# Involution stage: every second tap's multiply made one VectorE instruction of 1024 columns instead of two of 512

## The reference

```
r = relu(((x @ Wr + br) - mean) * rsqrt(var + eps) * gamma + beta)   # 16 channels
w = (r @ Ws + bs)                                   # 16 groups x 9 weights at each pixel
xi = x @ Wi + bi                                    # 64 channels, then padded by 1
patches[i, j] = xi_padded[i:i+32, j:j+32]           # 9 shifted copies
out = sum over the 9 taps of (w * patches), taken in the reference's own order of channels
x = x + out
```

## Time and profile before

| what | value |
|---|---|
| median of 3 runs | 677.94 us (677.34 to 678.18) |
| the profiled execution: its own time | 679.21 us |
| the profiled execution: span from first to last instruction | 677.4 us |
| PE busy | 647.1 us, 96% of the span |
| DVE busy | 552.7 us, 82% |
| ACT busy | 290.9 us, 43% |
| POOL busy | 172.4 us, 25% |
| mean granted TensorE clock | 0.980 of full speed |

### The profile page before, as it was taken

The page is one execution under the profiler, slowest core; times in us unless marked ns, Lnnn a source line. Parts: engine busy times, 40 slices in busy tenths (PEclk is TensorE's granted clock), DMA queues, the critical chain, the costliest instruction groups (busy, mean ns, idle before and its releaser), DMA issues.

```text
span 677.4 us, 14867 instructions
## 1 busy us (share of the span) xinstructions
PE 647.1 (96%) x6176; PEld 258.9 (38%) x6176; DVE 552.7 (82%) x904; ACT 290.9 (43%) x383; POOL 172.4 (25%) x156
## 2 busy tenths in 40 slices
PE   7868999899999999999999999999999999999995
PEld 7433333333333333333333334433444444444442
DVE  5699876979987988896486697848988888888885
ACT  3753622322322322132202310043688778778761
POOL 2100320008201900370032030321334234235230
PEclk9979999899999999999999999997999999999998
DMA  9930000000000000000000000000032132132132
GB/s 331 209 64 1 2 1 1 1 1 1 3 1 1 2 1 1 1 1 2 1 1 15 1 1 1 2 9 9 10 70 48 40 71 48 40 71 48 40 71 63
DMA packets 55119, 21.76 MB, mean 32 GB/s; under 512 B 51250, under 2 KB 51988, under 8 KB 55060
## 3 DMA queue, kind: packets, MB, share of 16 engines
q1 hardware_dynamic: 54772, 20.66, 12.4%
q10 hardware_dynamic: 288, 0.21, 0.1%
HBM read 10.38 MB, written 8.39 MB: 28 GB/s over the span
## 4 chain that ended last, share of the span: by engine, by line
PE 77%; DVE 12%; issue 1%; ACT 1%; DVEq 0%; ACTq 0%
PE conv L683 35%; PE conv L738 12%; PE att L754 11%; PE att L473 5%; PE conv L649 5%; DVE xpad L1199 3%; PE att L552 3%; PE att L564 2%; PE att L725 2%; DVE stats L1302 2%; DVE comb L1288 1%; PE att L531 1%; DVE x L1257 1%; DVE x L1264 1%; DVE x L1508 1%
## 5 line engine op out<-in xcount | busy, mean ns | idle before, releaser
L683 PE MATMUL conv<-xpad,comb 64*64 64x512 f32 x2592 | 290.2, 595 | 2.8 <-DVE x L1264 2.7
L1508 DVE TENSOR_TENSOR x<-conv,x 128x512 f32<-128x512 f32 x288 | 178.0, 683 | 24.1 <-PE conv L738 22.8
L683 PEld LDWEIGHTS conv<-xpad,comb 64*64 64x64 f32 x2592 | 98.5, 134 | 170.7 <-issue 160.1
L1288 DVE SCALAR_TENSOR_TENSOR comb<-experts,wsel,comb 128x576 f32<-128x576 f32 (+1 forms) x138 | 113.5, 888 | 5.2 <-ACT comb L866 4.8
L738 PE MATMUL conv<-rstack,wse 98*128 98x512 f32 x288 | 95.7, 437 | 1.7 <-DVE xin L1297 0.9
L866 ACT ACTIVATE comb<-experts,wsel 128x576 f32<-128x576 f32 (+2 forms) x49 | 35.2, 769 | 109.2 <-PE conv L683 69.7
L754 PE MATMUL att<-x,cmp 64*32 64x512 f32 x1280 | 80.5, 601 | 0.0
L738 PEld LDWEIGHTS conv<-rstack,wse 98*128 98x128 f32 x288 | 48.5, 190 | 70.6 <-DVE x L1508 63.9
L1199 DVE SCALAR_TENSOR_TENSOR xpad<-att,x 128x1024 f32<-128x1024 f32 x46 | 54.0, 1216 | 20.6 <-PE att L531 20.4
L1645 POOL TENSOR_TENSOR x<-x,xin 128x1024 f32<-128x1024 f32 x15 | 35.9, 2396 | 111.4 <-ACT x L1008 111.4
L876 ACT ACTIVATE x<-conv,bias 128x512 f32<-128x512 f32 x40 | 25.2, 681 | 83.8 <-PE conv L683 83.8
(11 more groups left out here) (187 smaller groups left out, 604.6 us busy)
## 6 DMA issues: line engine op xcount, KB each, us to landing
x<-in_x SPq DMA_DIRECT2D x32, 256.0 KB, 5.1
out<-comb SPq DMA_DIRECT2D x30, 256.0 KB, 3.2
rstack<-rstack SPq DMA_DIRECT2D x16, 128.0 KB, 3.8
experts<-in_We SPq DMA_DIRECT2D x1, 1152.0 KB
out<-comb SPq DMA_DIRECT2D x4, 128.0 KB, 2.2
wide<-in_c_wide SPq DMA_DIRECT2D x1, 192.0 KB, 6.6
x<-in_c_sum SPq DMA_DIRECT2D x1, 160.0 KB
small<-in_c_small ACTq DMA_DIRECT2D x1, 142.5 KB, 3.8
```

The lines of the kernel that those rows point to most:

```text
L683: last = nc.tensor.matmul(conv[own[to], h, HW * rows:HW * rows + HW], comb[own[rows], q % 2, n, tap(t)], xpad[own[rows], 2 * (q % 2) + n, ...
L1288: v.scalar_tensor_tensor(comb[:, q % 2, n, cols], experts[:, e, cols], wsel[:, p % 2, j + QP * n, e:e + 1], comb[:, q % 2, n, cols], ALU.m ...
L1508: v.tensor_tensor(img(prod[i])[:, rows, :], img(conv[:, unit, :])[:, rows, :], xip[s][:, kh + 16 * h:kh + 16 * h + 16, kw:kw + W], ALU.mul ...
```

## The change

`product` gets a second form for the odd taps (1, 3, 5 and 7). It waits until both halves of the unit are full, multiplies all 1024 columns in one instruction and raises `prod_ready` by 2 at its end. Even taps keep their two instructions of 512 columns. Nothing on the other engines is changed.

```
                 if not first:
                     eng.wait_ge(sum_done, (k - 1) * len(ROUNDS) + ROUND_OF[i] + 1)
+                if i % 2:
+                    eng.wait_ge(exp_full, 2 * e + 2)
+                    v.tensor_tensor(img(prod[i]), img(conv[:, unit, :]), xip[s][:, kh:kh + H, kw:kw + W], ALU.mult).then_inc(prod_ready, 2)
+                    return
                 for h in range(2):
                     rows = slice(16 * h, 16 * h + 16)
                     eng.wait_ge(exp_full, 2 * e + h + 1)
```

## The result

The changed kernel takes 680.88 us (median of 6 runs, 680.44 to 681.82), the kernel before 677.95 us (677.34 to 678.18): the ratio is 1.0049, 95% interval 1.0037 to 1.0060. That is +2.93 us; +2.65 was forecast. The profiled execution took 681.82 us with a span of 680.0, 2.6 more on both counts than the one before.

The account below looks back on a forecast made before the run. TensorE's own order was taken to bound the kernel. 2.15 us for pairs 2 to 14, 0.20 for pairs 1 and 15 and 0.3 for pair 0 gave 677.94 + 2.65 = 680.6 us, range 678.8 to 682.7.

Parts of the forecast that it names:

- Which engine sets the period: Middle pairs: TensorE's own order sets the 12.73 us; VectorE matters only where TensorE runs into one of its waits.
- The price of the merged product: VectorE, odd taps: a merged product takes 1.14 us of its time in place of 1.20, saving about 0.065 each.
- D: Time from start to release of a merged product on VectorE, taken as 1.215 us, bounds 1.162 to 1.330.
- The release: Tap 3's upper half comes 0.535 us later, so both tap 5 matmuls wait: next group +0.165 us a pair.
- the formula D - 1.05: How far the group after tap 5 moves in a middle pair, in us; +0.165 as forecast.
- The other odd taps: Taps 1, 5 and 7: later releases cost nothing while D stays under about 1.54; at least 0.33 us to spare.
- A middle pair's term: Pairs 2 to 14: each 0.165 us longer through the wait at tap 5, 2.15 us in all 13.
- Pair 1: Second pair of the last stage, where tap 1 and tap 3 are both late: forecast to cost +0.10 us.
- the start side: A merged product starts only when both halves are full: at tap 3 0.5 us is spare, so cost nothing.
- Faster, by VectorE's rate: Rival: VectorE's time is all on the path, 64 x 0.065 = 4.2 us go, 673.8 us; chance 0.07.
- No change, with ScalarE setting xi: Rival: ScalarE's release of xi's first load hides the lateness in middle pairs, 678.4 us; chance 0.13.
- Slower still, by stalls at tap 3 and tap 7: Rival: D over 1.54 makes tap 3 and tap 7 stall too, 684.9 us; chance 0.05.

Follow-up runs that it names:

- the long filler ahead of tap 7: Kernel before, plus a VectorE memset of 128x272 ahead of tap 7: 677.96 us, ratio 1.0000.
- The cut after 24 rows: Kernel before, with tap 3 cut after 24 image rows in place of 16, still two instructions: 678.12 us, ratio 1.0000.

## Why the prediction was right

*Which engine sets the period.* It was read from the waits and the chain, not from busy shares: VectorE was 87% busy in a middle pair (11.12 of 12.73 us) and still the time that the change saved there was worth nothing. The merges of taps 1, 5 and 7 show it without a cost in the way, and the long filler ahead of tap 7 shows that more of VectorE's time costs nothing there either. Ahead of tap 3 it does cost, one for one: VectorE counts where TensorE waits for it, as the prediction said.

*The price of the merged product.* D was taken as 1.215 us from a tensor_tensor in another stage; it is 1.215. From tap 3 to tap 4 VectorE went on after 558.99 - 557.86 = 1.13 us; 1.14 was taken.

*The release.* The load was expected 0.05 behind the product, two matmuls behind it 0.66, the idle stretch 0.5 to 0.6, taps 4 and 5 together 1.52: measured 0.05, 0.66, 0.57 and, by the loads, 1.53. The bound of 1.05 in the formula D - 1.05 is borne out from below too: an upper half that came free after 0.948 us changed nothing.

*The other odd taps* were costed at nothing with at least 0.33 us to spare. Merging them alone left a middle pair at 12.753 us.

*What was off in size.* A middle pair's term was 0.165 and measured 0.181, +0.2 us over 13 pairs; the difference of 0.016 is not taken apart. Pair 1 was given 0.10 and cost 0.26. Of the 0.16 by which it cost more, 0.13 is on the start side, which I had costed at nothing by the middle pairs alone: in pair 1 of the changed kernel tap 2's lower half starts at 479.53 and merged tap 3 only at 480.26, 0.73 later in place of 0.60.

```profile
479.53 0.68 DVE L1512 TENSOR_TENSOR x<-conv,x 128x512 f32<-128x512 f32 x1
...
480.26 1.23 DVE L1507 TENSOR_TENSOR x<-conv,x 128x1024 f32<-128x1024 f32 x1
```

Both of tap 3's matmuls were late there, since they had themselves waited for merged tap 1 (load at 479.07, after 0.94 us of idleness):

```profile
479.07 0.30 PEld L738 LDWEIGHTS conv<-rstack,wse 98*128 98x128 f32 x2 [0.94 <-DVE x L1507]
```

Their matmuls ended at 479.07 + 0.73 = 479.80, still ahead of the 480.13 at which VectorE would have come to tap 3 in step; what made it late are 0.40 us, from 479.87 on, that the chain shows as issue behind the wait. So in this one pair the wait for both halves did cost something. It takes both merges to get there: pair 1 took 14.05 us with tap 3 merged alone, 13.82 with taps 1, 5 and 7, and 14.17 with all four, against 13.91 before. Pair 0 cost 0.18 where 0.3 was forecast, and the last pair 0.09 for 0.10, but single executions differ too much in those parts for these two numbers to decide anything. That the parts add up to 2.6 us of span, so near to the 2.65, is in part luck: they were off by +0.2, +0.16, -0.12, -0.2 and, ahead of pair 0, -0.1.

*The rivals.* Faster, by VectorE's rate: out, by the three merges that cost nothing and gain nothing in the middle pairs. No change, with ScalarE setting xi: out, since the lateness came through; xi follows sum round 0 directly and takes 0.86 us as before, and a middle pair is 0.18 longer. Slower still, by stalls at tap 3 and tap 7: did not occur in the middle pairs.

From the fixed cost of an instruction that reads PSUM, 120 cycles in the Trainium skill's VectorE: DVE Perf Modes, section on the TRN2 errata, the prediction had an estimate of 0.125 us saved by each merge, which its sum did not use. The trace gives 1.20 - 1.13 = 0.07. The rule in the Trainium skill's Perfetto Trace Analysis, section Matmuls, is to rotate through banks so that evacuation overlaps the next matmuls. This case agrees with it in direction: tap 3's hand-over as one piece cost 0.18 us a pair. The cut after 24 rows shows where it made no difference, since there a hand-over 0.27 us later cost nothing; the merges of taps 1, 5 and 7 show the same.

**Is there a faster version?** None came out of the runs. The kernel before loses 1.36 - 1.13 = 0.23 us a pair at tap 5. Putting a sum round in front removed that wait, but one more change between expand and sum matmuls cost more: 12.880 against 12.744 us.

## What to carry to other kernels

Before two instructions are made one, ask who takes over the first one's buffer and how much work that engine has still to do behind it: the price is the lateness of the release plus the work that no longer overlaps, where the consumer already waits. Look for that place in the trace: here a single odd tap of four, whose release a load already awaited with 0.41 us of idleness, bore the whole cost of a middle pair, and the other merges were neutral. Time saved on an engine is worth nothing where that engine then only waits longer for another, even if it is busy for 87% of the time; the same engine's time counts in full ahead of a release that is waited for.

## What the hardware showed that I had not expected

- A product behind a short memset begins with it: both start at 544.45 where the memset of 128x32 lasts 0.09 us. That fits the products, which also start 0.08 us ahead of the reported end of the one before (0.68 us long, 0.60 apart), so 0.09 us of memset leave next to nothing. The memset of 128x272, 0.285 us long, did put tap 3's end off, by 0.23.
- Merging the first tap of a run costs more than merging the tap whose release is waited for: 0.246 against 0.177 us a pair, since VectorE then begins 0.31 us later, and tap 3 behind it is handed back later with both halves.
- A change from expand matmuls to sum matmuls and back costs TensorE about 12.880 - (12.744 - 0.23) = 0.37 us in this kernel, of which only about 0.20 is seen at the expand matmuls; the other 0.16 shows as 1.02 in place of 0.86 for the sum-type group behind them.
